# A decoder layer in fp32: cross-attention's exponentials transposed by DMA instead of by TensorE

## What is computed

```
x = x + _L0_attn_ref(_layernorm(x), qkv_w, qkv_b, out_w, out_b)
x = x + _L0_xattn_ref(_layernorm(x), ctx_1024, ctx_1024, mask, Wq, bq, Wk, bk, Wv, bv, Wo, bo)
x = x + _L0_ffn_ref(_layernorm(x), Win, bin_, W1, b1, W2, b2, Wout, bout)
# cross-attention, 16 heads of 32 values:
scores = jnp.einsum('bnlh,bnph->bnlp', qm, km) / np.sqrt(HEAD_DIM)
scores = jnp.where(mask, scores, MASK_FILL)
attn = jax.nn.softmax(scores, axis=-1)
out = jnp.einsum('bnlp,bnph->bnlh', attn, vm)      # then @ Wo.T + bo
# feed-forward: g = sum over 16 of relu(s * W1 + b1) * W2, then g @ Wout
```

## Time and profile before

| | |
|---|---|
| median of 3 runs | 1784.48 us (1783.67 to 1785.08) |
| profiled execution, its own time | 1784.44 us |
| span of its core | 1782.6 us |
| TensorE matmuls busy | 1685.4 us (95%) |
| VectorE busy | 1514.8 us (85%) |
| ScalarE busy | 1069.8 us (60%) |
| GpSimd busy | 1017.6 us (57%) |
| share of 16 DMA engines, queue q1 | 17.0% |

### The profile page before, as it was taken

One profiled execution on the slowest core, in us unless ns is written; L12 is line 12 of the kernel. 1 busy time (PEld: TensorE's weight loads), 2 busy tenths in 40 slices (PEclk: granted clock), 3 DMA queues, 4 the chain that ended last, 5 costly groups with the idle time before them and its releaser, 6 DMA issues.

```text
span 1782.6 us, 37666 instructions
## 1 busy us (share of the span) xinstructions
PE 1685.4 (95%) x13824; PEld 1392.6 (78%) x13824; DVE 1514.8 (85%) x2089; ACT 1069.8 (60%) x3420; POOL 1017.6 (57%) x721
## 2 busy tenths in 40 slices
PE   6899999999999999997799999999999999999996
PEld 5678888888888888885677787778777787777874
DVE  6788888888888888787678898888988899888886
ACT  4434444444443334442767788777877788777884
POOL 3267766666666666695554464545654465544521
PEclk9999999999999999998799999999999999999998
DMA  5410111111111111044201112011111112011101
GB/s 210 128 42 25 47 48 48 47 47 47 47 47 47 47 47 47 2 107 79 68 8 51 62 62 63 25 62 62 63 38 43 62 62 69 19 62 62 39 20 54
DMA packets 72793, 98.75 MB, mean 55 GB/s; under 512 B 22208, under 2 KB 30528, under 8 KB 72640
## 3 DMA queue, kind: packets, MB, share of 16 engines
q1 hardware_dynamic: 72064, 96.63, 17.0%
q10 hardware_dynamic: 576, 0.07, 0.0%
HBM read 59.66 MB, written 37.03 MB: 54 GB/s over the span
## 4 chain that ended last, share of the span: by engine, by line
PE 28%; ACT 12%; DVE 8%; issue 4%; DVEq 0%; POOL 0%; ACTq 0%; POOLq 0%
PE ring L1464 11%; ACT prob_c L1679 10%; DVE g_sb L1794 5%; PE sc L1492 5%; PE ring L1504 3%; PE ring L1469 3%; PE ring L1549 3%; PE sc L1484 2%; PE sc L1464 1%; DVE q_first L1975 1%; ACT relu L1660 1%; DVE g_sb L1791 1%; DVE gT L1803 1%; ACT gT L1669 1%; ACT pT L1648 0%
## 5 line engine op out<-in xcount | busy, mean ns | idle before, releaser
L447 PE MATMUL qb<-wqkv,xT 128*128 128x512 f32 x2304 | 551.9, 393 | 6.1 <-DVE wqkv L1016 6.1
L447 PEld LDWEIGHTS qb<-wqkv,xT 128*128 128x128 f32 x2304 | 429.7, 189 | 93.7 <-DVE wqkv L1016 6.3
L1679 ACT ACTIVATE prob_c<-sc,ntop 128x128 f32<-128x128 f32 x1024 | 362.6, 390 | 22.1 <-DVE ntop L1821 18.7
L1410 POOL TENSOR_TENSOR rstd<-vare,half_c 128x1 f32<-128x1 f32 x64 | 35.1, 549 | 433.6 <-DVE vare L1875 433.6
L1679 ACT ACTIVATION_READ_ACCUMULATOR prob_c<-sc,ntop 128x1 f32 x1024 | 236.1, 231 | 0.0
L352 POOL TENSOR_TENSOR prod_pool<-v,prob 128x1024 f32<-128x1024 f32 x64 | 179.9, 2810 | 67.8 <-DVE prob L911 62.6
L1464 PE MATMUL ring<-wqkv,aT_c 128*128 128x512 f32 x768 | 194.5, 402 | 8.0 <-DVE aT_c L1778 7.1
L663 ACT ACTIVATE v<-qb 128x512 f32<-128x512 f32 x64 | 38.3, 598 | 259.9 <-PE qb L447 249.6
L583 PE MATMUL ob<-wout,aT 128*128 128x512 f32 x768 | 191.4, 398 | 0.8 <-DVE aT L941 0.8
L1821 DVE TENSOR_REDUCE ntop<-sc 128x4 f32<-128x512 f32 x256 | 173.3, 683 | 12.3 <-PE sc L1492 9.5
L663 ACT ACTIVATE qk<-qb 128x512 f32<-128x512 f32 x128 | 76.1, 595 | 175.8 <-PE qb L447 175.8
(11 more groups left out here) (152 smaller groups left out, 3358.5 us busy)
## 6 DMA issues: line engine op xcount, KB each, us to landing
x_tile<-in_x SPq DMA_DIRECT2D x16, 1024.0 KB, 5.2
x_scratch<-xres SPq DMA_DIRECT2D x16, 1024.0 KB, 4.6
x_tile<-x_scratch SPq DMA_DIRECT2D x16, 1024.0 KB, 5.3
out<-x SPq DMA_DIRECT2D x64, 256.0 KB, 2.0
kt<-k_scratch SPq DMA_DIRECT2D x16, 512.0 KB, 3.2
v_c<-v_scratch SPq DMA_DIRECT2D x16, 256.0 KB, 3.6
raw<-in_wqkv SPq DMA_DIRECT2D x3, 1024.0 KB, 8.9
ctx<-in_ctx SPq DMA_DIRECT2D x1, 1024.0 KB, 8.3
```

The source lines that it names most:

```text
L447: last = nc.tensor.matmul(qb[g % 4][:, :], xT[p][a][:, k, t * P:(t + 1) * P], wqkv[b][:, k, c * D:(c + 1) * D], start=(n == 0), stop=(n == ...
L1679: last = nc.scalar.activation(prob[:, h, :], sc[g][:, (h % 4) * C:(h % 4 + 1) * C], ACT.Exp, bias=ntop[:, h:h + 1], accum_out=total[:, t % ...
```

## The change

The exponentials are split before they are transposed. `prob_hi` copies eight heads of `prob_c` (128x1024) as f16 into a new tile `p16_0` in SBUF, and `prob_lo` subtracts that from `prob_c` into `p16_1`: two instructions a tile on each engine in place of four. When both halves of a part are made, SyncE issues a transposing DMA of the whole part, 128 x 2048 f16 values (512 KB), into `pT0` or `pT1` (`turn`); the `values` of the tile wait for both transfers. `prob_T` and its turns in the ring go. The places in the queues differ from before: `prob_hi(t, 0)` stands behind the second group of exponentials and `prob_hi(t, 1)` behind the fourth, `prob_lo(t, 0)` ahead of `add_attn(t)` and `prob_lo(t, 1)` at the head of the next tile period. The exponentials of a group now wait until the same heads of the tile before are split (`p_lo`). `store(.., 3)` moves from the next step into its own.

```
 def slot_turns(t):
     if t == 0:
-        return [("out", 0), ("aT", 0), ("pv", 0), ("wo", 0), ("x2T", 0), ("pT", 0), ("pT", 1)]
+        return [("out", 0), ("aT", 0), ("pv", 0), ("wo", 0), ("x2T", 0)]
...
+        p16 = [sb(f"p16_{h}", [P, H, C], F16) for h in range(2)]
...
+            def turn(j, t):
+
+                n = 4 * j + t
+                for h, made in enumerate((p_hi, p_lo)):
+                    wait(sp, made, 2 * (n + 1))
+                    wait(sp, psum["pv"], n)
+                    sp.dma_start_transpose(pT[h][:, :, :],
+                                           p16[h][:, :, :].rearrange("p h c -> p (h c)")).then_inc(turned[h], 16)
...
-                if active(j - 1, "out", 3):
-                    store(j - 1, 1 - p, 3)
-                for t in range(R - 1):
+                for t in range(R):
+                    if t == 3 and has(j, 1):
+                        load_ctx(j + 1, 1 - p)
                     if active(j, "out", t):
                         store(j, p, t)
-                if has(j, 1):
-                    load_ctx(j + 1, 1 - p)
+                    if has(j):
+                        turn(j, t)
...
-                def prob_T(i):
-                    if not has(j):
-                        return
-                    g = i % 4
-                    wait(pe, exped, 16 * j + i + 1)
-                    dst = bank(j, ("pT", i))
-                    for h in range(4):
-                        last = nc.tensor.transpose(dst[:, h * P:(h + 1) * P], prob[:, 4 * g + h, :], ident[:, :])
-                    last.then_inc(psum["pT"], 1)
...
-                    wait(pe, taken["pT"], 4 * over)
+                    wait_each(pe, (turned[0], 16 * over), (turned[1], 16 * over))
...
-                    wait(act, psum["pT"], 16 * j + 4 * t - 3 + g)
+                    wait(act, p_lo, 2 * (4 * j + t - 1) + g // 2 + 1)
...
+                def prob_hi(t, part):
+
+                    n = 4 * j + t
+                    heads = slice(8 * part, 8 * part + 8)
+                    wait(act, exped, 4 * n + 2 * part + 2)
+                    if part == 0:
+                        wait(act, turned[0], 16 * n)
+                    nc.scalar.activation(p16[0][:, heads, :], prob[:, heads, :], ACT.Copy).then_inc(p_hi, 1)
...
+                def prob_lo(t, part):
+
+                    n = 4 * j + t
+                    heads = slice(8 * part, 8 * part + 8)
+                    wait(dve, p_hi, 2 * n + part + 1)
+                    if part == 0:
+                        wait(dve, turned[1], 16 * n)
+                    nc.vector.tensor_tensor(p16[1][:, heads, :], prob[:, heads, :], p16[0][:, heads, :],
+                                            ALU.subtract).then_inc(p_lo, 1)
```

More of the change, by code:

```diff
@@ L1173, in slot_turns @@
     if t == 0:
-        return [("out", 0), ("aT", 0), ("pv", 0), ("wo", 0), ("x2T", 0), ("pT", 0), ("pT", 1)]
-    late = [("pT", 4 * t - 2), ("pT", 4 * t - 1)]
+        return [("out", 0), ("aT", 0), ("pv", 0), ("wo", 0), ("x2T", 0)]
     if t < 3:
-        return [("aT", t)] + late + [("out", t), ("wo", t), ("pv", t), ("x2T", t), ("pT", 4 * t), ("pT", 4 * t + 1)]
-    return ([("aT", 3), ("xT", 0)] + late + [("wo", 3), ("xT", 1), ("out", 3), ("pv", 3), ("xT", 2), ("xT", 3),
-            ("pT", 12), ("pT", 13), ("x2T", 3)] + [("q", m) for m in range(DK)] + [("pT", 14), ("pT", 15)])
+        return [("aT", t), ("out", t), ("wo", t), ("pv", t), ("x2T", t)]
+    return ([("aT", 3), ("xT", 0), ("wo", 3), ("xT", 1), ("out", 3), ("pv", 3), ("xT", 2), ("xT", 3), ("x2T", 3)]
+            + [("q", m) for m in range(DK)])
 TURNS = [turn for t in range(R) for turn in slot_turns(t)]
@@ L1207, in active @@
 def active(j, kind, i):
-    shift = {"pv": -(i == 0), "aT": -(i < 2), "wo": -(i < 2), "x2T": -(i < 3), "pT": 0,
+    shift = {"pv": -(i == 0), "aT": -(i < 2), "wo": -(i < 2), "x2T": -(i < 3),
              "xT": 1, "q": 1, "s": -1, "out": -2}[kind]
@@ L1287, in cross_block @@
         ahead = keep["ahead"]
-        sb("bout_place", [P, D])
+        g_sb = sb("g_sb", [P, 4 * P])
         for name, shape, dt in CROSS_SMALL:
@@ L1319, in cross_block @@
         taken = {k: sem(f"taken_{k}") for k in TURNS_OVER}
-        hi = {k: sem(f"hi_{k}") for k in ("xT", "x2T", "aT", "pT", "q")}
+        hi = {k: sem(f"hi_{k}") for k in ("xT", "x2T", "aT", "q")}
         in_small = keep["in_small"]
@@ L1328, in cross_block @@
         scored, topped, exped, summed = sem("scored"), sem("topped"), sem("exped"), sem("summed")
+        p_hi, p_lo = sem("p_hi"), sem("p_lo")
+        turned = [sem(f"turned{h}") for h in range(2)]
         relu_done, hinged, g_hi, g_lo = sem("relu_done"), sem("hinged"), sem("g_hi"), sem("g_lo")
@@ L1682, in exps @@
                     last.then_inc(exped, 1)
-                def prob_hi(j, i):
-                    if not has(j):
-                        return
-                    g = i % 4
-                    if g == 0:
-                        wait(act, psum["pv"], 4 * j + i // 4)
-                    take_hi(j, "pT", i, pT[0][:, 4 * g:4 * g + 4, :])
+                def prob_hi(t, part):
[5 more added lines that the diff above has]
+                    nc.scalar.activation(p16[0][:, heads, :], prob[:, heads, :], ACT.Copy).then_inc(p_hi, 1)
                 def attn_hi(t, j=j):
@@ L1822, in tops @@
                                             AX.X, ALU.max, negate=True).then_inc(topped, 1)
-                def prob_lo(j, i):
-                    if not has(j):
-                        return
-                    heads = slice(4 * (i % 4), 4 * (i % 4) + 4)
-                    take_lo(j, "pT", i, pT[1][:, heads, :], pT[0][:, heads, :])
+                def prob_lo(t, part):
[6 more added lines that the diff above has]
+                                            ALU.subtract).then_inc(p_lo, 1)
                 def attn_lo(t, j=j):
@@ L1950, in step @@
                     tops(t, 3)
+                    prob_lo(t, 0)
+                    add_attn(t)
                     if t == 3:
```

53 lines of the change are left out of this document (9 added, 44 removed).

## The result

The changed kernel takes 1898.16 us (median of 4 runs, 1890.92 to 1904.05) against 1784.32 us (4 runs): ratio 1.0636, 95% interval 1.0591 to 1.0681, so 114 us slower. The forecast was slower, 1842 us, in a range of 1800 to 1975: the sign and the range hold. Of the other 56 us, the most is a term that is not in the sum, TensorE's clock, and the rest is a term of the tail that was put at nothing.

A forecast was written before the change was run, and what follows sets the result against it. A loop through ScalarE, 9.94 us a tile, was taken as the bound, with VectorE closing a second. Three periods at +0.95 and tile 0 at +1.0 make 3.85 us a step, +58 over 15 steps: 1842 us, range 1800 to 1975.

The forecast's parts named there:

- What goes: Cross stage: TensorE loses 16 transposes a tile, costed at nothing because the scores wait for ScalarE at every E.
- rival (c): Faster: cheaper copy and subtraction (0.5 and 0.6 us) give a 9.2 us period, 1754 us; chance 0.09.
- The loop in tiles 1 to 3: Cross-stage tile period goes from 9.94 to 10.9 us, +0.95 in each of three periods a step.
- VectorE's loop: Early subtraction, add_attn, rtotal to vare, then the next late subtraction: 10.15 us a tile before the GpSimd price.
- E: Moment at which ScalarE has done a tile's last exponential; first exponential forecast to move from E+3.17 to E+3.6.
- The price of meeting GpSimd: VectorE's subtractions with two SBUF operands wait out GpSimd's instructions: 0.36 us each (0.65 x 0.56), bounds 0 and 0.65.
- Tile 0: First tile period of a step: a pT copy now stands among its exponentials, +1.0 us.
- The tail: Hinges and query products ending a step: queries at E+3.5 to E+3.9 against 3.85 before, costed at nothing.
- Rival (a): Transfers exposed: at D = 4.3 a 12.1 us period, 1930 us, 1870 to 2020 for D 3.3 to 6; chance 0.28.
- the likeliest case: Slower with transfers hidden: 1808 to 1870 us, its lower edge without waiting for GpSimd; chance 0.50.
- D: Time of a 512 KB transposing transfer beyond 1.1 us fixed: taken as 2.6 us, hidden; it decides from 3.1.
- rival (b): Transfers bound everything: 67 ns a packet, D = 8.6, a tile takes 19.65 us, 2370 us in all; chance 0.08.

The follow-up runs named there:

- Experiment 2: Kernel before with one transpose of exponentials instead of four for each bank, result partly wrong: 1802.26 us, ratio 1.0106.
- experiment 1: Changed kernel plus useless transposes on TensorE in its gaps, 16 a tile in the mean: 1872.78 us, ratio 1.0513.
- experiment 7: Changed kernel with tile 0's first ScalarE copy moved behind its last exponential: 1911.53 us, ratio 1.0729.
- Experiment 4: Changed kernel with VectorE's early subtraction behind add_attn (and the output's addition in the last period), not ahead: 1879.23 us, ratio 1.0540.
- experiment 5: Changed kernel without the transposing transfers, the products with v taking a constant: 1893.09 us, ratio 1.0605.
- experiment 8: Changed kernel with the low part's transfer made twice, the second behind the first's landing: 2022.43 us, ratio 1.1340.

## Why the forecast was right in its sign and 56 us short

**What goes: TensorE's time at nothing.** This is the step that failed. It said that time freed on TensorE "becomes idle time in front of" the scores, and so costs nothing. It did become that, and idle time was the cost: after it TensorE runs at 1.2 GHz for a while, and then its matmuls are on the loop. Experiment 2 shows this by the removal alone (+19 us, +1.06%), experiment 1 by the reverse (25 us back for more work). The prediction read "at a granted clock of 1.00" in the earlier trace rows beside 97 of 100 us busy, and did not ask whether the clock would stay at 1.00. Its rival (c) even took TensorE's relief as an argument for faster. The sum lacks this term: some 40 us by what is left over, of which 25 are shown.

**The loop in tiles 1 to 3.** The forecast had 10.9 us a tile. At a clock of 1.00 (experiment 1) tiles 1 and 2 take 10.63 and 11.06: the size is right, and so is the loop. It came as 10.15 for VectorE's loop plus 2 x 0.36 for GpSimd; the late subtractions of the kernel after mostly stand 10.96 apart in tile 2 at full clock, of which 0.88 is GpSimd's (2.10 less 1.22), so 10.1 without. Pieces agreed too: the copy took 1058 ns (forecast 1.0), the subtraction alone 1.21 (1.2), and the maximum follows the x2T subtraction without a gap. The first exponential starts at E + 4.2, not 3.6: E is 1318.09 and the exponential starts at 1322.28, as this row shows.

```profile
1318.09 1.06 ACT L1675 ACTIVATE p<-prob_c 128x1024 f16<-128x1024 f32 x1
...
1322.28 0.37 ACT L1663 ACTIVATE prob_c<-sc,ntop 128x128 f32<-128x128 f32 x1 [0.66 <-DVE ntop L1796]
```

The late subtraction did not start at E + 1.05, when its copy was done, but at E + 1.74, when the statistics ahead of it on VectorE were. That is where VectorE's loop held, as forecast.

**The price of meeting GpSimd.** Forecast 0.36 us a subtraction, 0.65 in 56 cases of 100. Measured 0.15 in the mean of all 128: 1367 ns, against a median of 1224 and a longest of 2252. That mean is not what counts. On the loop of tiles 1 and 2 the early subtraction pays 0.4 in the mean and 0.88 in the rows above, more than the upper bound of 0.65, and the late one nothing (1217 ns), except that of tile 0, which stands at the head of tile 1's period (1464). Together that is 0.7 us in tile 1 and 0.45 in tile 2, against 0.72: near as a sum, but divided otherwise than forecast, so part of it is luck. At the late subtraction the meeting fell on the other side: `rstd` on GpSimd took 0.55 us in the earlier trace rows and has a median of 1462 now, as in this row beside the subtraction that starts at 1319.83.

```profile
1319.99 1.46 POOL L1418 TENSOR_TENSOR rstd<-vare,half_c 128x1 f32<-128x1 f32 x1 [4.76 <-DVE vare L1854]
```

The two start 0.16 us apart and GpSimd's ends 0.41 us after VectorE's. The Trainium skill ("SBUF — State Buffer", SBUF: two separate sides) says that a VectorE operation with two operands in SBUF and a GpSimd one that reads SBUF take a shared pair of ports for a whole instruction, whoever starts first. By that rule the trace agrees in the main: a wait from 1319.99 to the subtraction's end would add 1.05 us, and 0.91 is added to an operation of 0.55. It agrees the other way round too, where the early subtraction starts second and ends 1.1 us behind GpSimd's.

**Tile 0.** Forecast +1.0, from the copy between its exponentials. Measured 8.86 to 9.87, and experiment 7 shows the cause.

**The tail.** Forecast: its queries at nothing, and 0.95 for tile 3's period. Measured +2.0 at full clock, 28.3 to 30.3. Tile 3's period, to its last exponential, has 0.8 of that (10.83 to 11.63 in experiment 1). The rest is the queries: at full clock they start at E + 5.15 in the mean, not at E + 3.5 to 3.9, against 3.8 before. This is the other step that failed. Here E is 1341.10:

```profile
1341.10 1.06 ACT L1675 ACTIVATE p<-prob_c 128x1024 f16<-128x1024 f32 x1
1343.66 1.22 DVE L1806 TENSOR_TENSOR p<-prob_c,p 128x1024 f16<-128x1024 f32 x1
1344.80 1.28 DVE L1753 TENSOR_TENSOR xT_c<-ring,xT_c 128x512 fp32r<-128x512 f32 x2
1346.14 4.25 PE L1472 MATMUL ring<-xT_c,wqkv 128*128 128x512 f32 x17 [0.42 <-DVE xT_c L1753]
```

The prediction's three subtractions fit E + 3.5 only if the late one starts when its copy is done, at E + 1.05. But in VectorE's order the statistics stand ahead of it, behind the early subtraction, and they end at E + 2.6 (in the kernel before, at E + 1.1); the xT subtractions and the queries follow. The prediction had followed just this row on VectorE in its loop and did not in the tail.

A bank adds to it: the ring turn of `norm_T(2)` is freed by `add_attn(3)`, which the early subtraction of 1.2 us delays. Experiment 4 shortens this wait, which is worth some 0.4 us a step at full clock; its queries still start at E + 5.2. No run moved the statistics, so this cause is read from the rows and not tested.

**The transfers.** Rival (a), exposed transfers, would have given 1930 us and lies nearer to the time than the forecast does; it is nevertheless not the cause: experiment 5 removes them for 5 us. The range reached to 1975 because of it, and 1898 lies above the 1870 at which the likeliest case ended, so that the range held is partly luck. D itself can't be read apart. One landing takes 4.6 us, and the formula with 1.1 fixed and D = 2.6 gives 3.7. SyncE needs a median of 2.1 us to issue each one, which no row of before could show. Room was forecast as 0.5 us (D = 2.6 against 3.1); by experiment 8 it is 0.6 to 1.5 or more. Of rival (b) the packets came true, some 2080 a transfer, and their price did not: q1's time rose from 17.0% of 1782.6 us to 36.2% of 1902.2, an estimated 23 ns for each new one and not 67. The load of x_tile was needed sooner than the prediction said, since GpSimd waits for it in each step, but that cost nothing (experiment 5). The Trainium skill ("Advanced Engine Details and Errata", X-Bar Transpose (TRN2)) has transposes as fast as regular DMAs. The trace neither bears this out nor refutes it: a plain one of 512 KB, from DRAM, landed in 3.2 us, this one, within SBUF, in 4.6, but the plain one was issued in 0.33 us and this one in 2.1, and from the end of the issue it is 2.9 and 2.4 us. The difference is in the issue.

**The sum, again.** Forecast 3.85 us a step; measured 4.9 at full clock, the queries of the tail being most of the difference. With that, 74 us; and 40 of clock.

## What to carry to other kernels

Before you cost freed TensorE time at nothing, look at the granted clock and at how full TensorE is: where the loop runs through its matmuls, idle time may be paid for in slower matmuls, and a version with work left out of the kernel before (experiment 2) measures this by itself. When an instruction is put ahead of others on an engine, list everything behind it and what each frees, banks included, and do it for every stage: the missed 1 us of the tail was the statistics behind the early subtraction, which the forecast had counted in the tile periods. A chain of waits names one path where two end close together: look at what the next instruction in the engine's own order was doing before you name the loop. And an engine that only hands over (here the DMA engines, 0.5 to 0.6 busy in the cross stage) can be innocent though it is the new thing in the profile: take it out and time it before you blame it.

## What the runs showed of the hardware

- Useless TensorE work in the gaps made the kernel 25 us faster (1898 to 1873), with the granted clock over the run 0.976 in place of 0.924.
- A transposing transfer of 512 KB kept SyncE's queue for a median of 2.1 us (1.3 to 4.7) and landed after 4.6 (4.2 to 6.7), counted from the start of the issue; a plain one of that size kept it for 0.33 and landed after 3.2. The queue's packets rose from 72064 to 338304, some 2080 a transfer, and its share from 17.0% to 36.2%.
- GpSimd's operation on 128x1 went from 548 to a median of 1462 ns when VectorE's two-operand subtraction had started just before it. The other way round, that subtraction went from 1.22 to 2.10 us when it started inside a GpSimd operation on 128x512.
